# A fused transformer-and-state-space kernel: the multiply of u by a spread row of B moves from GpSimd to VectorE

## The reference

```
dt = softplus(dt_raw * w + b)          # [t, d]
dA[t,d,n]  = exp(dt[t,d] * A[d,n])
dBx[t,d,n] = (dt[t,d] * x[t,d]) * B[t,n]
h[t,d,n]   = dA[t,d,n] * h[t-1,d,n] + dBx[t,d,n]
y[t,d]     = sum over n of h[t,d,n] * C[t,n]
```

## Time and profile before

| | |
|---|---|
| median of 3 runs | 2514.21 us (2509.17 to 2514.93) |
| the profiled execution | 2515.7 us from its first to its last instruction |
| VectorE busy | 2154.8 us, 86% |
| TensorE matmul busy | 1786.1 us, 71% |
| GpSimd busy | 1118.2 us, 44%, of which the multiply by B 719.0 us |
| ScalarE busy | 1035.9 us, 41%, of which the copy of B 151.3 us |
| mean granted TensorE clock | 0.844 of full speed |

### The profile page before, as it was taken

The page is one execution under the profiler, slowest core; times in us unless marked ns, Lnnn a source line. Parts: engine busy times, 40 slices in busy tenths (PEclk is TensorE's granted clock), DMA queues, the critical chain, the costliest instruction groups (busy, mean ns, idle before and its releaser), DMA issues.

```text
span 2515.7 us, 24789 instructions
## 1 busy us (share of the span) xinstructions
PE 1786.1 (71%) x6433; PEld 982.1 (39%) x6433; DVE 2154.8 (86%) x3132; ACT 1035.9 (41%) x1722; POOL 1118.2 (44%) x602
## 2 busy tenths in 40 slices
PE   4776104346787887877787878787878787878687
PEld 3454003312344444444344434443444444444344
DVE  4888791139899998999999999999999999999996
ACT  1322000135463545454545444454545354636343
POOL 1101306724556454554455545555454445454540
PEclk7999555567898889898898888898888889989899
DMA  6333102300000000000000000000000000000000
GB/s 168 100 106 98 27 1 39 37 17 8 5 5 9 5 9 5 8 4 9 5 9 4 9 5 9 4 13 1 13 0 13 1 13 0 13 1 5 5 1 9
DMA packets 72565, 49.75 MB, mean 20 GB/s; under 512 B 5296, under 2 KB 68432, under 8 KB 72144
## 3 DMA queue, kind: packets, MB, share of 16 engines
q1 hardware_dynamic: 57872, 39.85, 5.5%
q0 software_dynamic: 14592, 8.92, 2.8%
HBM read 27.50 MB, written 21.18 MB: 19 GB/s over the span
## 4 chain that ended last, share of the span: by engine, by line
DVE 35%; PE 26%; issue 22%; POOL 11%; ACT 2%; DMA 1%; SPq 1%; DVEq 1%; POOLq 0%; ACTq 0%
DVE hst L1330 8%; PE bank L906 7%; DVE prod L1343 5%; POOL dbx L528 5%; PE bank L915 3%; PE bank L917 3%; DVE prod L1348 3%; DVE hg L1253 3%; PE bank L934 2%; DVE hh L1266 2%; PE bank L949 1%; DVE cand L1154 1%; DVE val L1157 1%; POOL rwp L506 1%; PE bank L862 1%
## 5 line engine op out<-in xcount | busy, mean ns | idle before, releaser
L528 POOL TENSOR_TENSOR dbx<-u,bs 128x1024 f32<-128x1024 f32 x256 | 719.0, 2818 | 363.9 <-ACT bs L670 232.1
L1330 DVE TENSOR_TENSOR_SCAN hst<-dA,dbx 128x1024 f32<-128x1024 f32 x256 | 675.7, 2639 | 26.2 <-issue 14.6
L906 PE MATMUL bank<-prod,ident 128*128 128x512 f32 x832 | 490.3, 720 | 79.3 <-DVE prod L1348 58.0
L678 ACT ACTIVATE dA<-dt,aneg 128x511 f32<-128x511 f32 x512 | 338.2, 709 | 17.3 <-DVE hst L1330 15.2
L1343 DVE TENSOR_TENSOR prod<-hst,bank 128x1024 f32<-128x1024 f32 x256 | 310.4, 1213 | 19.4 <-PE bank L894 11.2
L670 ACT ACTIVATE bs<-bank 128x512 f32<-128x512 f32 x256 | 151.3, 591 | 338.2 <-PE bank L890 335.4
L906 PEld LDWEIGHTS bank<-prod,ident 128*128 128x128 f32 x832 | 183.3, 226 | 258.3 <-issue 154.7
L691 ACT ACTIVATE ht<-hg 128x512 f32<-128x512 f32 (+1 forms) x208 | 130.8, 629 | 309.5 <-DVE hg L1253 308.3
L915 PE MATMUL bank<-x3T,w_w 128*128 128x512 f32 (+1 forms) x416 | 230.1, 636 | 0.7 <-ACT x3T L696 0.7
L894 PE MATMUL bank<-parts,sel_bc 99*128 99x512 bf16 x256 | 107.6, 420 | 166.0 <-DVE prod L1343 164.2
L917 PE MATMUL bank<-x3T,w_w 128*128 128x512 f32 (+1 forms) x416 | 213.9, 596 | 0.1
(11 more groups left out here) (202 smaller groups left out, 2529.6 us busy)
## 6 DMA issues: line engine op xcount, KB each, us to landing
xg_rows<-xg SPq DMA_DIRECT2D x16, 320.0 KB, 2.5
xt<-in_x SPq DMA_DIRECT2D x16, 256.0 KB, 3.1
xT<-in_xT SPq DMA_DIRECT2D x16, 256.0 KB, 3.4
resid_rows<-zero SPq DMA_DIRECT2D x16, 256.0 KB, 3.4
resid_rows<-resid SPq DMA_DIRECT2D x16, 256.0 KB, 2.4
rin<-resid_rows SPq DMA_DIRECT2D x16, 256.0 KB, 2.8
rin<-resid_rows POOLq DMA_DIRECT2D x16, 256.0 KB, 4.8
out_dram<-ofin SPq DMA_DIRECT2D x16, 256.0 KB, 2.4
```

Source lines behind the costliest of these rows:

```text
L528: gp.tensor_tensor(dbx[n % 2][:, :, :], u[s.par][:, :, :], bs[n % 2][:, :].rearrange("p (h t) -> p h t", h=1).to_broadcast([P, NH, SEQ]), ...
L678: act.activation(dA[n % 2][:, h, 1:SEQ], dt_[s.par][:, h, 1:SEQ], ACT.Exp, scale=aneg[:, h, n:n + 1]).then_inc(da_rdy, 1)
L906: last = mm(y_ps[:, h, :], ident[:, :], prod[n % 2][:, h, :], start=(sums_to(n) == 1), stop=(n == NS - 1), skip_group_check=True)
L1330: dve.tensor_tensor_scan(flat(hst[n % 2]), flat(dA[n % 2]), flat(dbx[n % 2]), 0.0, ALU.mult, ALU.add).then_inc(scan_rdy, 1)
```

## The change

GpSimd's `spread_u` and ScalarE's `copy_b` are gone, with the tiles `bs` and the semaphore `bs_rdy`. VectorE gets its own `spread_u`, which reads bank 2 where it lies. Who takes bank 2 after a row of B now waits for `dbx_rdy`, the multiply, where it waited for `bs_rdy`, the copy. The pieces of the diff stand in the order GpSimd, ScalarE, TensorE (two), VectorE (the last three).

```
-            def spread_u(s, n):
-                if n == 0:
-                    gp.wait_ge(u_rdy, s.at(1, 1))
-                gp.wait_ge(bs_rdy, s.at(NS, n + 1))
-                need(gp, scan_rdy, s.at(NS, n - 1))
-                gp.tensor_tensor(dbx[n % 2][:, :, :], u[s.par][:, :, :],
-                                 bs[n % 2][:, :].rearrange("p (h t) -> p h t", h=1).to_broadcast([P, NH, SEQ]), ALU.mult
-                                 ).then_inc(dbx_rdy, 1)
...
-                    if s and n < NS - 1:
-                        spread_u(s, n + 1)
-                    if f and n == NS - 1:
-                        spread_u(f, 0)
...
-            def copy_b(s, n):
-                act.wait_ge(bb_rdy, s.at(NS, n + 1))
-                need(act, dbx_rdy, s.at(NS, n - 1))
-                act.activation(bs[n % 2][:, :], pa_ps[:, :], ACT.Copy).then_inc(bs_rdy, 1)
...
             def spread_b(s, n):
-                turn(pa_ps, bs_rdy, s.at(NS, n + 1))
+                turn(pa_ps, dbx_rdy, s.at(NS, n + 1))
...
                 if s:
-                    held["a"] = (bs_rdy, s.at(NS, 2))
+                    held["a"] = (dbx_rdy, s.at(NS, 2))
...
+            def spread_u(s, n):
+                if n == 0:
+                    dve.wait_ge(u_rdy, s.at(1, 1))
+                dve.wait_ge(bb_rdy, s.at(NS, n + 1))
+                need(dve, scan_rdy, s.at(NS, n - 1))
+                tt(dbx[n % 2][:, :, :], u[s.par][:, :, :], over_h(pa_ps), ALU.mult).then_inc(dbx_rdy, 1)
...
                         tt(prod[n % 2][:, :, :], hst[n % 2][:, :, :], over_h(cb_ps), ALU.mult).then_inc(prod_rdy, 1)
+                    if s and n < NS - 2:
+                        spread_u(s, n + 2)
...
                     if o:
                         tail(o, n)
+                    if f and n >= NS - 2:
+                        spread_u(f, n + 2 - NS)
```

More of the change, by code:

```diff
@@ L211, in build @@
         dt_ = [sb(f"dt{p}", [P, NH, SEQ]) for p in range(2)]
-        bs = [sb(f"bs{p}", [P, SEQ]) for p in range(2)]
         u = [sb(f"u{p}", [P, NH, SEQ]) for p in range(2)]
@@ L282, in build @@
         ld_r, f_mv, f_rs = sem("ld_r"), sem("f_mv"), sem("f_rs")
-        x2_rdy, x2T_mm, x2T_rdy, cv_mm, bs_rdy = sem("x2_rdy"), sem("x2T_mm"), sem("x2T_rdy"), sem("cv_mm"), sem("bs_rdy")
+        x2_rdy, x2T_mm, x2T_rdy, cv_mm = sem("x2_rdy"), sem("x2T_mm"), sem("x2T_rdy"), sem("cv_mm")
         cv_rdy = sem("cv_rdy")
@@ L719, in iteration @@
                         scan_step(f, 0)
[L720 to L723, removed]
                     if o and n < TAIL:
```

## The result

The changed kernel takes 2600.7 us (2599.5 to 2607.5, four runs) where the kernel before took 2514.2; the ratio is 1.035 (95% interval 1.033 to 1.037). Forecast was 2553 us, range 2510 to 2588. The direction was right, the size was not: +86 us instead of +39. The profiled execution has a span of 2605.8 us. One further execution of the kernel before, 2596.9 us at over 1.5% above its others, is a slow one and is left out.

The account below looks back on a forecast made before the run. VectorE, busy 2154.8 of 2515.7 us, was taken as the bound, partly standing still behind GpSimd's SBUF reads. The terms 289 - 242 - 16 + 21 - 39 - 10 + 36 = +39 us gave 2553 us, range 2510 to 2588.

Parts of the forecast that it names:

- VectorE stands still while GpSimd reads SBUF, 242 us due to the product: Scan stage: two-SBUF-operand VectorE instructions stall while GpSimd reads SBUF; removing GpSimd's product gives back 242 us.
- The multiply at 1.13 us of room: VectorE, scan stage: 256 new multiplies with one PSUM operand, 1.13 us each like `prod`, add 289 us.
- Work added less hold-ups removed: VectorE: 289 us of multiplies, less 242 of hold-ups by GpSimd's product and 16 by `u`.
- The wait for u: Step 14: the multiply waits 1.3 us for GpSimd's `u`, 16 times, 21 us.
- Gates no longer wait for L917, 39 us: VectorE before `hg`: two multiplies between `prod` and gate cover TensorE's chain, so 38.8 us of waits go.
- Step 7, the transposed routing weights: Transposition L969 waits for the multiply, TensorE starts 1.4 us later, step 9's gate gap grows to 2.6 us: 36 us.
- The sign that was named: Profile after: gap before `hg` in step 9 of 2 to 3 us in nearly all sequences, almost nowhere else.
- The exception is step 7: Bank 2 is held until VectorE's multiply; in most steps its next user finds it free, except in step 7.
- Rival 3: TensorE becomes the bound at bank 2's eight hand-overs a sequence, 0.4 us each, 48 us on top: 2601 us; chance 0.12.
- the signs that the rival named: Gaps at `hg` in steps 5, 10 and 11 would mark rival 3.
- the forecast's items: VectorE's waits: +21 for `u`, +36 for step 7's bank hand-over, -39 before gates, -10 before scans.
- the forecast's sum without bank 2, 2517: The sum without the 36 us for step 9's gate, as if TensorE catches up: 2517 us; chance 0.18.

Follow-up runs that it names:

- Experiment 5: Multiply cut to 16 of 1024 columns, waits kept: GpSimd's in the kernel before, 2273.9 us (ratio 0.905); VectorE's in the changed kernel, 2335.1 us (0.932).
- experiment 7: Kernel before, with GpSimd's multiply for state n + 2 held until VectorE has done `hs` of step n: 2431.3 us, ratio 0.970.
- experiment 6: Changed kernel with VectorE's multiply for state n + 2 ahead of `prod` of step n instead of behind it: 2587.0 us, ratio 1.025.
- experiment 1: Changed kernel with ScalarE's copy of the row of B put back and VectorE multiplying by the copy: 2546.8 us, ratio 1.015.
- experiment 2: Changed kernel with two users of bank 2, l1 and `rwT`, moved to bank 7: 2541.7 us, ratio 1.015.
- experiment 4: Changed kernel with ScalarE's copy of B kept and both l1 and `rwT` moved to bank 7: 2545.2 us, ratio 1.016.

## Why the prediction was right in direction and wrong in size

- *VectorE stands still while GpSimd reads SBUF, 242 us due to the product:* shown. All groups named fell to near their shortest durations, the scan but for y2. Experiment 5 puts the price at 233 us, and experiment 7 gets 81 us back by moving nothing but GpSimd's starts. One thing the prediction passed over: its words are of two SBUF operands, but x3 and `ofin`, which it priced (42 and 25 us), read one SBUF tensor and two columns of scalars, and they were held up as well (1026 and 781 ns, 339 and 341 without the product).
- *The multiply at 1.13 us of room:* shown, 1213 ns as `prod`. Work added less hold-ups removed was forecast at 31 us and is 30.
- *The wait for u:* 21 us forecast, 13.3 measured in the changed kernel, because TensorE is late for the gate before it and takes that part; in step 14 the two are 10.8 and 10.8 us, and where TensorE is in time the wait for `u` is 22.6 (experiment 6). From one sequence:

```profile
1515.76 0.75 DVE L1229 SCALAR_TENSOR_TENSOR hg<-bank,w_b,ha 128x512 f32<-128x512 f32 x1 [0.72 <-PE bank L893]
...
1517.76 1.22 DVE L1249 TENSOR_TENSOR dbx<-u,bank 128x1024 f32<-128x1024 f32 x1 [0.65 <-POOL u L536]
```

- *Gates no longer wait for L917, 39 us:* mostly wrong. The waits of steps 5 and 12 went but for 0.6 us (6.1 and 12.9 us before), but 30.7 us of waits before `hg` are left in the stage, in steps 6, 9 and 14, and 35.5 us of waits for the row of B came beside them, in steps 2, 6 and 9; the sum had no item for these. The slack of two multiplies is there only while TensorE's chain starts at `prod`; in steps 6 and 9 it starts at VectorE's release of bank 2.
- *Step 7, the transposed routing weights:* right in mechanism and near in size, 2.6 us forecast and 3.1 measured in the sequence above, but split over `hs`, the multiply and `hg`. The sign that was named, gaps before `hg` in step 9 of 2 to 3 us and almost nowhere else, did not come: none there is over 0.6 us. The old gap was read well enough, 16.2 us in 15 sequences, though the gate at 2050 us that I called the last is followed by one of 1.65 at 2172. I had followed TensorE's queue to the gate and not ScalarE's, where `ht` stands behind the reads of z. The item was 36 us; moving `rwT` gives back 30 (plus or minus 11).
- *"The exception is step 7":* this is the step that failed. l1 in step 5 also takes bank 2 behind the multiply, and its result comes back to VectorE in the same step. By the forecast's items VectorE's idle time in steps 5 and 6 would be 13.6 us (20.9 less 7.3 of waits before `hg`); it is 51.7, and moving l1 alone makes it 12.5. That hand-over, put at nothing, is 38 of the 47 us of idle time that the forecast lacks. In step 5 the slack is between the multiply and its own successor, `hg`, which gives 0.66 us of room, and TensorE needs 1.88 for l1, at the 1.2 GHz level behind 2.79 us of idle time.
- *Rival 3 has the measured time, 2601 us, by luck.* It put 0.4 us for each of eight hand-overs on top of the forecast and had a chance of 0.12, because there was "at least one multiply of slack" outside step 7. In the traces l1's hand-over alone has 39 us of idle time, 2.6 a sequence, and the signs that the rival named, gaps at `hg` in steps 5, 10 and 11, are 0.6 us in all. It was right only in that l1 is in its list.

The account closes in the traces. From its first `dt` on VectorE's idle time went from 130.3 to 185.1 us, +55, where the forecast's items give +21 + 36 - 39 - 10 = +8. Of the difference of 47, steps 5 and 6 have 38 and steps 7 to 9 have 8 (46.9 us, where the items give 20.3 - 16.2 - 1.4 + 36 = 38.7); the rest nearly cancels. With 30 us of busy time that is 85. The two profiled executions are 90 us apart, and the other 5 to 6 us lie before the first `dt` (at 551.1 us, and at 545.5 in the kernel before); the other kernels have it between 539.8 and 545.4, and nothing lays this to the change.

Open: the kernels of experiments 1, 2 and 4 are still 35 us by ratio, 25 to 30 by their medians, above the forecast's sum without bank 2, 2517. In the trace of experiment 2 VectorE idles 20 us longer than the remaining items give, 14 of them in steps 7 to 9 and 5 in step 12, before `hs`, rows and `hg`; that they come from z, x_proj and the parts in the same bank is argued from the order, not tested.

## What to carry to other kernels

An engine that is busy less than half and that hardly anybody waits for can still cost 233 us: hold the mean duration of each group against its shortest before calling a second engine's work free, and try to move its start to where the neighbour's instructions don't mind before moving the work. When a reader of a shared PSUM bank moves to a busy engine, list every user that takes the bank after it and follow each through all three queues back to that engine; a user whose result is wanted in the same step pays the full loop. A copy that nobody waits for may be what frees the buffer.

## What the runs showed of the hardware

GpSimd's y2 (2.36 us from 1495.00) and the scan beside it (4.15 us from 1495.36) end as if run one behind the other. The reverse holds: in the kernel before a product has 2.37 us at the median and 4.49 at the longest, which is one whose scan came 0.06 us behind it and kept its own length:

```profile
2241.67 4.49 POOL L528 TENSOR_TENSOR dbx<-u,bs 128x1024 f32<-128x1024 f32 x1
```

```profile
2241.73 2.28 DVE L1330 TENSOR_TENSOR_SCAN hst<-dA,dbx 128x1024 f32<-128x1024 f32 x1
```

By the records GpSimd began first both times; behind y2 it is the scan that stands still, and here the product. `prod`, `hg` and `hh` keep their lengths beside a product (experiment 7). TensorE's eight small matmuls of l1 took 0.95 us straight behind other work, at a granted clock of 1.00, and 1.88 us behind 2.79 us of idle time, at 0.50.
